# A new place in the written order for the last sequence's steps, and for the projection of the one ahead of it, in a two-layer attention kernel

## The reference

```python
x = x + xattn(layernorm(x), ctx, ctx, lens, Wq, Wk, Wv, Wo)      # 16 heads of 32, 77 keys with a mask
x = x + ffn(layernorm(x), ...)                                    # a self-attention with mixed weights
# ffn, for each sequence b:
#   gates, top_idx = softmax of the two best of 8 experts, from the mean over the tokens
#   q, k, v, out = x @ Wm.T + sum over 2 experts of gate * ((x @ V.T) * S) @ U.T + bias
#   attn = softmax(q k^T * 32**-0.5) over 512 keys, 16 heads;  ctx = attn @ v;  out from ctx
```

## Time and profile before

| | |
|---|---|
| runs | 1449.62, 1446.61, 1447.97 us; median 1447.97 |
| the profiled execution's own time | 1451.72 us |
| its span, first to last instruction | 1449.9 us |
| mean granted TensorE clock | 0.971 of full |
| busy: PE, DVE, ACT, POOL | 1397.0, 952.5, 862.0, 681.1 us |
| DMA queue q1 | 128.66 MB, 33.2% of 16 engines' span |

### The profile page before, as it was taken

How to read it: one execution, slowest core, us unless ns; L and a number is a source line. 1 busy time by engine, 2 the same in 40 slices (tenths; PEclk the granted TensorE clock), 3 DMA queues, 4 the chain that set the end, 5 groups by cost and what they waited for, 6 DMA issues and landing times.

```text
span 1449.9 us, 17120 instructions
## 1 busy us (share of the span) xinstructions
PE 1397.0 (96%) x5688; PEld 700.9 (48%) x5688; DVE 952.5 (66%) x1687; ACT 862.0 (59%) x1499; POOL 681.1 (47%) x411
## 2 busy tenths in 40 slices
PE   6999999999999999999999999999999999899886
PEld 4545544544454554545455554545455554444332
DVE  4464577767766777767766777767767676766532
ACT  2426474866487664866578663866577663756441
POOL 2022143556455462546446462545446462567463
PEclk9989989999999999999999999999999999999967
DMA  6533233522533224522523224522423222422300
GB/s 213 155 108 95 50 69 102 136 74 49 141 80 91 71 58 116 150 75 45 136 76 104 70 57 118 150 74 45 125 83 103 74 54 80 132 59 55 77 28 29
DMA packets 78239, 130.81 MB, mean 90 GB/s; under 512 B 26358, under 2 KB 31094, under 8 KB 75079
## 3 DMA queue, kind: packets, MB, share of 16 engines
q1 hardware_dynamic: 74055, 128.66, 33.2%
q10 hardware_dynamic: 4096, 1.06, 0.3%
HBM read 66.08 MB, written 12.21 MB: 54 GB/s over the span
## 4 chain that ended last, share of the span: by engine, by line
PE 86%; ACT 5%; DMA 2%; issue 2%; POOL 2%; SPq 1%; DVE 1%; ACTq 0%; POOLq 0%; DVEq 0%
PE pj L1099 43%; PE scT L1184 9%; PE acc L1213 8%; PE sc L1156 7%; PE sc L1145 3%; PE pj L1129 2%; PE scT L1177 2%; PE pj L1193 2%; PE pj L1201 2%; PE pj L1222 2%; PE pj L1093 2%; ACT xhat L707 1%; PE pj L1074 1%; ACT qs L790 1%; PE pj L1085 1%
## 5 line engine op out<-in xcount | busy, mean ns | idle before, releaser
L822 ACT ACTIVATE probs<-scT 128x512 f32<-128x512 f32 x512 | 289.3, 594 | 315.3 <-PE scT L1184 311.3
L938 DVE TENSOR_REDUCE negmax<-sc 128x1 f32<-128x512 f32 x512 | 338.0, 684 | 148.8 <-PE sc L1156 148.0
L685 POOL TENSOR_TENSOR probs_sum<-probs_sum,probs 128x1024 f32<-128x1024 f32 x128 | 300.1, 2369 | 61.0 <-ACT probs L822 61.0
L1156 PE MATMUL sc<-ks,qs 96*128 96x512 f32 x512 | 262.6, 547 | 5.8 <-DMA ks<-ks 2.5
L965 DVE RECIPROCAL inv_sum<-pj 128x128 f32<-128x128 f32 x256 | 224.9, 921 | 64.2 <-PE pj L1222 26.2
L1184 PE MATMUL scT<-qs,ks 99*128 99x512 f32 x512 | 254.4, 526 | 8.4 <-ACT probs L822 5.6
L1099 PE MATMUL pj<-XT,Wqk 128*128 128x512 f32 x512 | 256.4, 597 | 0.0
L681 POOL TENSOR_TENSOR probs_sum<-probs 128x1024 f32<-128x1024 f32 x64 | 151.5, 2373 | 191.5 <-ACT probs L822 191.5
L1184 PEld LDWEIGHTS scT<-qs,ks 99*128 99x128 f32 x512 | 97.0, 195 | 130.5 <-ACT probs L822 62.1
L691 POOL TENSOR_TENSOR uv_stack<-UVS_sb,uv_stack 96x1024 fp32r<-96x1024 f32 x32 | 75.6, 2364 | 174.0 <-ACT UVS_sb L729 174.0
L1156 PEld LDWEIGHTS sc<-ks,qs 96*128 96x128 f32 x512 | 97.8, 193 | 96.8 <-issue 52.5
(11 more groups left out here) (101 smaller groups left out, 1723.0 us busy)
## 6 DMA issues: line engine op xcount, KB each, us to landing
Wqk<-in_WmT SPq DMA_DIRECT2D x16, 1024.0 KB, 8.0
Wvo<-in_WmT SPq DMA_DIRECT2D x16, 1024.0 KB, 5.7
UVS_sb<-in_UVS SPq DMA_DIRECT2D x64, 192.8 KB, 3.3
qs<-stage_lo SPq DMA_DIRECT2D x136, 64.0 KB, 2.3
qs<-qs SPq DMA_DIRECT2D x34, 256.0 KB, 3.1
X<-in_x SPq DMA_DIRECT2D x8, 1024.0 KB, 5.7
ks<-stage_lo SPq DMA_DIRECT2D x128, 64.0 KB, 2.0
ks<-ks SPq DMA_DIRECT2D x32, 256.0 KB, 3.0
```

Source lines behind the costliest of these rows:

```text
L685: nc.gpsimd.tensor_tensor(probs_sum[:, pair], probs_sum[:, pair], probs[:, kt % 2, pair], ALU.add)\
L822: nc.scalar.activation(probs[:, kt % 2, jj, :], scT[:, ST[step], :], ACT.Exp, scale=SCALE)\
L938: nc.vector.tensor_reduce(negmax[:, 0, n:n + 1], sc[:, SC[step], :], AX.X, ALU.max, negate=True)\
L1156: nc.tensor.matmul(sc[:, SC[step], :], qs[0:3 * DH, slot, jj, t * P:(t + 1) * P], ks[0:3 * DH, slot, jj, :], start=True, stop=True).then_i ...
```

## The change

Only the table `OWN` changes; no instruction is added or taken away. It gains numbers for nearly all later steps of sequence 7 and for the projection of sequence 6, and the numbers of sequence 7's output matrix, `out2` and `residual2` are other ones. All other steps keep theirs. As before, a number says only what a step stands ahead of.

```diff
@@ OWN @@
-    "context_v": {(0,): -1382},
-    "wm_load": {(7, 3): 20464, (0, 0): -185, (0, 1): -287, (0, 2): 597},
-    "uv_load": {(7, 3): 15834, (0, 0): 322, (0, 1): 354, (0, 2): 475},
-    "uv_hi": {(7, 3): 20376, (0, 0): 354, (0, 1): 473, (0, 2): 584},
-    "uv_lo": {(7, 3): 25932, (0, 0): 404, (0, 1): 491, (0, 2): 627},
-    "weff": {(7, 3, 0): 31424, (7, 3, 1): 32766, (7, 3, 2): 36119, (7, 3, 3): 39486, (0, 0, 0): 422, (0, 0, 1): 441,
+    "context_v": {(0,): -1382, (7,): 12774},
+    "wm_load": {(7, 3): 18708, (0, 0): -185, (0, 1): -287, (0, 2): 597, (7, 1): 14706, (7, 0): 14531, (7, 2): 14385},
+    "uv_load": {(7, 3): 15449, (0, 0): 322, (0, 1): 354, (0, 2): 475, (7, 2): 14841, (7, 0): 14576, (7, 1): 14699},
+    "uv_hi": {(7, 3): 18360, (0, 0): 354, (0, 1): 473, (0, 2): 584, (7, 1): 14767, (7, 2): 14851, (7, 0): 14606},
+    "uv_lo": {(7, 3): 18563, (0, 0): 404, (0, 1): 491, (0, 2): 627, (7, 1): 14786, (7, 2): 14880, (7, 0): 14616},
+    "weff": {(7, 3, 0): 19360, (7, 3, 1): 19558, (7, 3, 2): 19761, (7, 3, 3): 20656, (0, 0, 0): 422, (0, 0, 1): 441,
...
-    "out2": {(7, 0, 0): 51874, (7, 0, 1): 56365, (7, 0, 2): 57135, (7, 0, 3): 57237, (7, 1, 0): 58327,
-        (7, 1, 1): 58791, (7, 1, 2): 59098, (7, 1, 3): 59483, (7, 2, 0): 59665, (7, 2, 1): 60562, (7, 2, 2): 61119,
-        (7, 2, 3): 61480, (7, 3, 0): 61545, (7, 3, 1): 61559, (7, 3, 2): 62948, (7, 3, 3): 64057},
-    "residual2": {(7, 0): 58491, (7, 1): 60860, (7, 2): 63065, (7, 3): 65452},
+    "out2": {(7, 0, 0): 20650, (7, 0, 1): 21042, (7, 0, 2): 21535, (7, 0, 3): 22325, (7, 1, 0): 21864,
+        (7, 1, 1): 21908, (7, 1, 2): 22105, (7, 1, 3): 22609, (7, 2, 0): 23827, (7, 2, 1): 23835, (7, 2, 2): 23856,
+        (7, 2, 3): 23872, (7, 3, 0): 23286, (7, 3, 1): 23303, (7, 3, 2): 23372, (7, 3, 3): 24203, (6, 0, 0): 15587,
+        (6, 0, 1): 15787, (6, 0, 2): 16019, (6, 0, 3): 16619, (6, 1, 0): 17085, (6, 1, 1): 17430, (6, 1, 2): 17666,
+        (6, 1, 3): 17984, (6, 2, 0): 18028, (6, 2, 1): 18046, (6, 2, 2): 18113, (6, 2, 3): 18249, (6, 3, 0): 18541,
+        (6, 3, 1): 18573, (6, 3, 2): 18590, (6, 3, 3): 18642},
+    "residual2": {(7, 0): 22429, (7, 1): 22906, (7, 2): 24453, (7, 3): 24950, (6, 0): 16670, (6, 1): 18035,
+        (6, 2): 18453, (6, 3): 19456},
...
+    "shift": {(7, 0): 15606, (7, 1): 18277, (7, 2): 19738, (7, 3): 20530},
+    "shift_move": {(7, 0): 15635, (7, 1): 18303, (7, 2): 19756, (7, 3): 20542},
...
+        (7, 3, 1): 18394, (7, 1, 1, 0): 18817, (7, 1, 1, 1): 18983, (7, 1, 2, 0): 19142, (7, 1, 2, 1): 19290,
...
+    "accout": {(7, 0): 18747, (7, 1): 19953, (7, 2): 20646, (7, 3): 21990},
+    "den": {(7, 0): 18507, (7, 1): 19738, (7, 2): 20740, (7, 3): 21892},
+    "inv": {(7, 0, 0): 18525, (7, 0, 1): 18582, (7, 0, 2): 18583, (7, 0, 3): 18610, (7, 1, 0): 19759,
+        (7, 1, 1): 19802, (7, 1, 2): 20531, (7, 1, 3): 20655, (7, 2, 0): 21026, (7, 2, 1): 21249, (7, 2, 2): 21301,
+        (7, 2, 3): 21339, (7, 3, 0): 21946, (7, 3, 1): 22235, (7, 3, 2): 22310, (7, 3, 3): 22676},
+    "divide": {(7, 0, 0): 18986, (7, 1, 0): 20855, (7, 2, 0): 21354, (7, 3, 0): 22067, (7, 3, 1): 22391,
+        (7, 3, 2): 23543, (7, 3, 3): 24079},
```

41 lines of the change are left out of this document (26 added, 15 removed), and 81 rows, old and new, of the table OWN.

## The result

The changed kernel took 1428.30 us (median of four runs, 1425.79 to 1429.29), the kernel before on the same chip 1448.26 us (1446.61 to 1449.62). The ratio on record is 0.9859, with a 95% interval of 0.9845 to 0.9873: some 20 us less, where 16.0 was forecast. (Such a ratio is not the quotient of the two medians, which is 0.9862 here. By the medians the gain is 20.0 us, by the ratio 20.4.

The account below looks back on a forecast made before the run. TensorE bounds the middle; at the end, waits and the low clock level cost up to some 34 us. 13.0 - 0.5 + 2.0 + 1.5 = 16.0 us off the 1447.97 median gives 1432.0 us, range 1424 to 1442.

Parts of the forecast that it names:

- rival 2: All of it: full clock level throughout, no new waits; 22.4 us gained, 1425.6 us; chance 0.12.
- A: Last `den` to last product: only twelve products remain, no `weff`; 11.5 to 15.0 us gained, 13.0 taken.
- The timing of the quarters: Behind the last `den`, job 3's divided quarters come every 0.85 us, as fast as products ask for them.
- the argument for the better end: Three products and a `den` more in job 3 hand a full clock to the end: 15.0 us gained.
- the row: Profile row in job 3: clock at half from 1405 to 1410 though TensorE was busy 4.40 of 5 us.
- B: Job 3: POOL's `divide` of job 2 joins the chain to `den`; nothing to 5.9 us lost, 0.5 taken.
- the prediction's sign: Job 3: POOL's six `psum` with one `divide` within take 15.9 us from first to last without gaps.
- C: Job 2's first `sT` to job 3's: the two `pv` no longer adjacent; 0 to 4.4 us gained, 2.0 taken.
- rival 3: Slower: finer mixing keeps the clock at half from job 2's `sT` on; 1453 us; chance 0.03.
- D: Jobs 0 and 1, and steps moved there: 1.0 us lost to 3.0 gained at waits, 1.5 taken.
- Rival 1: Only the end is won, clock at half through job 3; 5.6 to 7.1 us gained; chance 0.20.
- Rival 4: No difference: POOL's chain sets the end, 13 to 19 us of new waits; 1445 to 1451 us; chance 0.03.

Follow-up runs that it names:

- e1: Kernel before with only sequence 7's output matrix formed early, all sixteen products still behind the last `den`: 1439.42 us, ratio 0.9934.
- e4: e1 plus the change's end (`divide` of job 2 earlier, four products into job 3, order of the last twelve): 1436.46 us, ratio 0.9908.
- f2_fill_end: Kernel before with 27 small products of constants in the 6.49 us wait for `uv_lo` at the end, nothing moved: 1447.23 us, ratio 0.9988.
- g1: The change with `divide` of job 2 done by DVE instead of POOL: 1427.11 us, ratio 0.9845.
- g3: g2 with reciprocals and `divide` of job 2 directly behind its `den` on DVE, ahead of the additions: 1426.45 us, ratio 0.9851.
- e3: Kernel before's order up to job 2's `shift`, from there the order of e2: 1444.97 us, ratio 0.9972.
- e2: The change with sequence 7's weights, products, residuals and last divides put back to the end: 1443.09 us, ratio 0.9957.
- f1: e3 with ten small products of constants filling two TensorE waits in job 2: 1444.33 us, ratio 0.9977.
- u3: The change with `den` of job 2 put back ahead of job 3's first two `sT`: 1427.03 us, ratio 0.9849.
- g4: g3 with job 2's last `sc` moved ahead of the last product of job 3's keys: 1428.68 us, ratio 0.9854.
- g2: g1 with three of POOL's six `psum` of job 3 also moved to DVE: 1424.31 us, ratio 0.9826.
- a2: The change again without an edit, on the chip of the third set of runs: 1426.55 us, ratio 0.9857.

## Why the prediction was right, and where it was short

The sign, the size class and the place were right: faster by 20 us of 1448, at the upper edge of the forecast of 12 to 20, most of it behind the last `den`. The profiled pair, with 22.6 us, came out as rival 2 (22.4 us), which had 0.12; that is in part chance, as the execution before was 3.5 us over its median and the one after 0.8. By its own steps:

**A, the end: right, at its better end.** The range was 11.5 to 15.0 and 13.0 was taken; 14.4 was measured. Twelve products took 10.92 us, which is the full level from the first on (10.2 was worked out from 0.853 each). The timing of the quarters held too: TensorE's products are one row without an idle time, so none came late. What was left open between the ends was the clock, and it was full: 1.00 from 1413 to 1418. In e1, without the products in job 3, it was 0.81 in the first 4.8 us, in e4, with them, 1.00, which is what the argument for the better end had said. e1 and e4 split the piece into 10.4 us for the weights and 4.0 for the products moved ahead. The Trainium skill ("TensorE: Matmul & The Clock Gate", "What's actually happening"), which was set against the row, says that activity releases the low level. That agrees with this trace at the end of the program (1.00 from 1413 to 1418) and with f2_fill_end (0.68 up to 1423, 1.00 from there to 1427, within the fill); by it alone the term was 15.0 us.

**B, job 3: right in size, and the reason given holds in the change.** A loss of 0.5 us was taken and 1.0 measured; both are of the size of the scatter. The reason, POOL's 1.28 us on the chain to `den`, is shown by g1 (1.0 us come back) and by g3 (4.6 us come back when half of POOL's additions and this `divide` leave it). Against the kernel before it did not cost its full length: POOL's row there had a gap of 0.73 us, and from its first addition to its last it took 14.7 us, where it now takes 15.2 (the prediction's sign was 15.9). The other half of the loss is a first addition that comes 5.6 us behind the first `sT` instead of 5.1. In e4, with the same `divide` in the same place, B was 20.6, less than before, so the loss is no fixed price of the `divide`. TensorE's own wait of 1.78 us for this `divide`, and the products and the `pv` behind it, stand beside that chain: the two end together, POOL at 1412.02 and the `pv` at 1412.07.

**C, job 2: the step that failed.** The prediction said: "Ends: 0 and 4.4 us gained; I take 2.0, nearest POOL's row." It was 8.6. The mechanism named was there: ACT's wait behind the two `pv` has shrunk from 4.35 us to 1.60 at most, and the order from the `shift` on gives 4.0 us by itself (e3 against before), close to the upper end; against f2, whose order is the old one too, it gives 2.8. The prediction's own sign, 22 to 26 us from job 2's first `sT` to job 3's, was missed with 18.0. Two things had no price in the sum:

1. *The clock within the piece.* A, B and rival 3 were worked out at two levels, C at none. Yet its own rows showed the half level: two `pv` in 3.64 us. With the level at 1.00 the same work takes TensorE 13.4 us instead of 17.6, and in the stretch up to job 3's `shift` e3 against e2 puts this part at 3.4 us and f1 against e3 at 2.6, each by one pair of profiles. From the rows it could have been priced at 4.0: 17.6 us of TensorE's time at 0.77 are 13.6 at the full level. The upper end of C should have been 4.4 + 4.
2. *A waiting step ahead of others on its engine.* That `den` of job 2 "now stands behind two `sT`" was said under C, to exclude a cost. It was also a gain, since in the kernel before it stood ahead of them: put back there (u3), the piece is 2.6 us longer, and the way to the last `den` 2.2 us. In the pair itself, the way from job 3's `shift` to its first `sT` is 4.6 us before and 3.3 after, 1.3 us of the 8.6.

These overlap, and e3 holds the second of them already, so they are not to be added to its 4.0. From profile to profile, 4.0 (before to e3, the order), 4.2 (e3 to e2: 3.4 with the level, the rest the longer issue) and 0.4 (e2 to the change) make the 8.6.

The wait for the keys' stack (1.74 us), said to stay, has gone. Not because the keys came sooner: the `shift` itself waits 1.89 us for DVE, whose maximum stands behind a `weff` addition and a split, and the `den` and `pv` behind it run at the half level (1.61 and 2.01 us), so TensorE comes later to the same keys: from the last key product to the first `sc` of job 3 it is 10.2 us before (1367.18 to 1377.34) as after.

**D, jobs 0 and 1: right in sign, the size open.** 1.5 us was taken, 0.6 measured in this pair. From the first `shift` of sequence 7 to job 2's first `sT` it is 60.2 us instead of 64.2, but that `shift` comes 3.4 us later, with more work ahead of it and within the scatter told of above. The wait of 1.13 us is gone: from that `shift` to the first `sT` of job 1 it is 35.3 us in every profile with the change's order, 38.4 in every one with the old. Job 2's first `sT` comes at 1370.4 us in the mean of the eight profiles with the change's order up to there (1367.6 to 1374.9), and at 1373.8 in the mean of the six with the old (1370.1 to 1377.0). That is 3.4 us and not 0.6, within wide scatter, so this pair may have put into C what belongs to D. `uv_hi`, `uv_lo` and the load of `Wvo` found their covers: POOL's `uv_lo` waits for `uv_hi` until 1348.30, but its next addition has to wait for exponentials until 1353.82 anyway, and DVE's additions to `Wvo` wait for no transfer.

**Rival 1** (only the end is won, at the half level) is refuted for the change by the clock of 0.93 in the last 50 us and by the order's 6.2 us (e2). **Rival 3**, the clock at half through finer mixing, is refuted at 0.93 in the last 75 us, though part of job 2 did fall back to the half level in g4 and g1 (0.82 and 0.81 in the stretch), behind waits. **Rival 4**, new waits that give the gain back, found its waits, but 1.89, 1.78 and 1.02 us of TensorE are 4.7 us, where it needed 13 to 19.

What stays open: why single profiles differ upstream, which limits what four to ten runs can tell here to some 2 to 5 us, so that g2 and g3 are neither shown to beat the change nor to equal it. Open too is how much of C's clock part is the order's doing: in the stretch of job 2 the level was at 0.99 or more in seven of the ten profiles with the change's order there (one of them filled, f1) and below in three (e3, g1, g4); with the old order it was at 0.77 to 0.84 in all four. One profile of each kernel says little of how often.

## What to carry to other kernels

- Price every piece of the bound engine at both of its levels, and let the better level be an end of the term: what closes a wait of 1 to 2 us may also win the clock for the 15 us behind it. Here some 3 of C's 8.6 us went with it, by single profiles.
- In an in-order queue, ask of each step that waits what stands behind it: two ready `sT` behind a `den` that waited for POOL cost 2.2 us.
- When the last stage waits for inputs that don't depend on it, form these early into the other engines' idle times. That was 9.6 of 20.4 us, and with four products moved into the stage ahead 13.3, two thirds of the gain. The first part could be read from one wait of 6.49 us and the four `weff` behind it.

## What the runs showed of the hardware that was not expected

**Less waiting is not always less time.** The change's order gave 14.6 to 14.8 us for job 2's stretch in five profiles (after, a2, g2, g3, u3), and 17.9 in g1, whose steps up to there are the same. In g1, TensorE ran the `den` behind the `shift` at the full level (1.07 us), came to the transfer before that had landed, stood for 0.45 and then 1.03 us, and was granted 0.81:

```profile
1364.76 1.07 PE L1322 MATMUL pj<-probs_sum,ones 128*32 128x512 f32 x8 [0.50 <-POOL probs_sum L776]
...
1367.56 0.73 PE L1284 MATMUL scT<-qs,ks 99*128 99x512 f32 x2 [0.45 <-DMA qs<-shift]
...
1370.76 0.47 PE L1256 MATMUL sc<-ks,qs 96*128 96x512 f32 x1 [1.03 <-DMA ks<-ks]
```

In the change that `den` ran partly at the half level (1.61 us, and 1.80 to 1.94 in the other four), no wait for a transfer above 0.21 us followed, and the level was full for the whole stretch. Being 1.0 us faster into the job went with 3.2 us more in it. What decides which of the two happens was not tried.

**The level can be half at a high busy share.** It was half in g4 with TensorE busy for 4.88 of 5 us, and in e3 for all of 4.00, behind waits of 1.7 to 2.2 us; in f1, with 16 short instructions in the place of the wait, it was 1.00.

**DVE's additions beside POOL's.** With both operands in the on-chip memory, an addition of 128x1024 took DVE 1.22 us in g2 when POOL had nothing to do, and 2.25 and 1.70 us beside one of POOL's; a multiplication of 128x512 took 0.69 us alone (g2) and 2.20 in g3, begun while POOL was adding. POOL's own additions kept to 2.35 to 2.37 us in g2 and g3, but for one of 2.67 in g3, and a pair that took 4.68 us in the change took 5.14 in g1, with DVE's multiplication beside it (2.20 us). The Trainium skill ("SBUF — State Buffer", "Who interferes with whom") says that a DVE instruction with two SBUF inputs contends with a GpSimd instruction that reads SBUF, and that the order of issue decides which of them is blocked. These rows agree, as if DVE had begun when POOL's addition ended: 1394.28 + 2.37, the end of POOL's addition in g3, is 1396.65, and 0.69 us before the multiplication ends at 1397.20 is 1396.51. So work taken from POOL to DVE costs more there than its time alone, as long as POOL goes on.
